# Three graph layers over sorted edges: chunks that begin at any stored record, and table steps written out

## The reference, cut to what matters

```
def _spmm(row, col, vals, x):
    msg = vals[:, None] * x[col]
    return jax.ops.segment_sum(msg, row, num_segments=N)

def _layer(x_prev, row, col, vals, W_a, b_a, W_b, b_b):
    h = _spmm(row, col, vals, x_prev)
    z = (h + x_prev) @ W_a.T + b_a + h * x_prev @ W_b.T + b_b
    return jnp.where(z >= 0, z, NEG_SLOPE * z)

x = emb[x_ids]; x1 = _layer(x, ...); x2 = _layer(x1, ...); x3 = _layer(x2, ...)
return jnp.concatenate((x, x1, x2, x3), axis=1)
```

## Time and profile before

| | us |
|---|---|
| median of 3 runs | 10225.11 (10217.66 to 10225.59) |
| profiled execution, its own time | 10220.25 |
| its span, first to last instruction | 10218.3 |
| TensorE matmuls busy | 9241.7 (90%) |
| VectorE busy | 8226.2 (81%) |
| GpSimd busy | 5098.6 (50%) |
| ScalarE busy | 4417.4 (43%) |
| mean granted TensorE clock | 0.92 |

### The profile page before, as it was taken

How to read it: one execution, slowest core, us unless ns; L and a number is a source line. 1 busy time by engine, 2 the same in 40 slices (tenths; PEclk the granted TensorE clock), 3 DMA queues, 4 the chain that set the end, 5 groups by cost and what they waited for, 6 DMA issues and landing times.

```text
span 10218.3 us, 236191 instructions
## 1 busy us (share of the span) xinstructions
PE 9241.7 (90%) x72184; PEld 8455.2 (83%) x72185; DVE 8226.2 (81%) x11648; ACT 4417.4 (43%) x13845; POOL 5098.6 (50%) x2843
## 2 busy tenths in 40 slices
PE   6788886788888669999999999999999999999999
PEld 4567665466676549999999999989999999999999
DVE  7899998699999857777777777777777777777777
ACT  0577775067777516652111256641111466511112
POOL 8477775057777500006888600028888200088885
PEclk8788887778888759999999999999999999999999
DMA  2111111011111299998888889998888699988885
GB/s 74 35 6 6 6 6 18 6 5 6 6 6 6 23 61 344 344 335 295 284 286 286 252 277 341 340 313 285 286 286 286 224 344 347 336 282 286 286 286 210
DMA packets 1121792, 1969.65 MB, mean 193 GB/s; under 512 B 390740, under 2 KB 442008, under 8 KB 1121080
## 3 DMA queue, kind: packets, MB, share of 16 engines
q0 software_dynamic: 399392, 1034.26, 32.8%
q1 hardware_dynamic: 722328, 934.52, 30.9%
HBM read 1212.58 MB, written 755.66 MB: 193 GB/s over the span
## 4 chain that ended last, share of the span: by engine, by line
PE 48%; DVE 20%; DMA 15%; issue 10%; ACT 3%; SPq 1%; DVEq 1%; POOL 0%; ACTq 0%; POOLq 0%
PE ps L912 35%; DMA messages<-work 14%; PE ps L903 7%; DVE hT L1102 7%; DVE place L1081 7%; DVE hT L1096 3%; ACT work L670 3%; PE ps L746 1%; PE ps L883 1%; PE ps L940 1%; PE ps L920 1%; PE ps L941 1%; PE ps L768 1%; DVE place L1086 0%; DVE place L1084 0%
## 5 line engine op out<-in xcount | busy, mean ns | idle before, releaser
L511 POOL DMA_INDIRECT work<-messages,work x1920 | 2923.1, 1522 | 3687.7 <-issue 3686.8
L912 PE MATMUL ps<-work 128*128 128x125 f32 x30720 | 3548.7, 278 | 38.3 <-DVE work L1279 38.3
L912 PEld LDWEIGHTS ps<-work 128*128 128x128 f32 x30720 | 3504.3, 192 | 82.7 <-DVE work L1279 39.4
L486 POOL DMA_INDIRECT sorted_edges<-stage,run_idx x798 | 1968.5, 2467 | 1286.1 <-ACT stage L615 570.9
L903 PE MATMUL ps<-xb,work 125*128 x21504 | 2459.2, 277 | 149.0 <-DVE work L1251 80.3
L903 PEld LDWEIGHTS ps<-xb,work 125*128 125x128 f32 x21504 | 2425.6, 193 | 182.6 <-issue 182.1
L1279 DVE TENSOR_TENSOR work<-work,iota_p 128x1000 f32<-128x1000 f32 x1920 | 2291.5, 1193 | 34.7 <-ACT work L688 34.7
L670 ACT ACTIVATE work<-ps,work 128x128 f32<-128x128 f32 x5376 | 1515.5, 372 | 1264.9 <-DMA messages<-work 648.5
L688 ACT ACTIVATE work<-work 128x8 f32<-128x8 f32 x1920 | 577.7, 301 | 2880.4 <-DMA work<-messages,work 2880.4
L796 PEld LDWEIGHTS ps<-hT 128*128 128x128 f32 x12768 | 1694.7, 215 | 69.4 <-issue 46.5
L626 ACT ACTIVATE hT<-iota_p,place 128x128 f32<-128x128 f32 x4788 | 1427.9, 386 | 707.7 <-DVE place L1086 699.7
(11 more groups left out here) (201 smaller groups left out, 3820.8 us busy)
## 6 DMA issues: line engine op xcount, KB each, us to landing
messages<-work SPq DMA_DIRECT2D x2688, 256.0 KB, 6.2
work<-slot_cols SPq DMA_DIRECT2D x672, 256.0 KB, 6.0
work<-messages,work POOLq DMA_INDIRECT x1920, 5.9
out_x<-xb SPq DMA_DIRECT2D x150, 125.0 KB
sorted_edges<-stage,run_idx POOLq DMA_INDIRECT x798, 3.7
work<-lane_places SPq DMA_DIRECT2D x532, 5.2 KB
out_x<-xb SPq DMA_DIRECT2D x4, 1562.5 KB
sorted_edges<-hT SPq DMA_DIRECT2D x4, 908.0 KB
```

The source lines that it names most:

```text
L486: pool.indirect_dma_start(out=sorted_edges[p], out_offset=bass.IndirectOffsetOnAxis(ap=run_idx[:, q, k:k + 1], axis=0), in_=stage[:, q, k ...
L511: pool.indirect_dma_start(out=ck[:, n, :, :].rearrange("p h x -> p (h x)"), out_offset=None, in_=octs, in_offset=bass.IndirectOffsetOnAxis ...
L912: last = t.matmul(part[n], ck[:, n, j // CH, j % CH * D:(j % CH + 1) * D], sel[:, n % SELB, j, :], start=j == 0, stop=j == CHB - 1)
```

## The change

- A chunk may begin at any stored record. The messages are seen as rows of 4 floats (`flat`), and ScalarE multiplies the chunk's index, now counted in records, by 129 (REC // CH) when it copies it. Each gather still brings 128 pieces of two records. The number of chunks of a pair is its number of records touched, halved and rounded up; the table counts records, the step from chunk to chunk is HALVES = 2, the limit of the `min` is CHUNKS in place of OCTS.
- A column block's groups in the second pass keep room for 4 more slots (`p * CH`), so that a chunk's second record is never another block's first. The number of groups stays at 896.
- TB becomes 592.
- Differences in the chunk table are split in three parts (4096, 64, 1) in place of two.
- The steps of both run tables are written out on VectorE and TensorE, with constant addresses, in four buffers (SCREDIT = 4). The steps of the chunk table are written out too, 296 steps of CR = 2 tiles in CQ = 2 buffers, in place of 128 steps of 5.

The diff, changed lines only:

```diff
@@ -49,6 +49,7 @@
+SCREDIT = 4
@@ -80,18 +81,18 @@
-OCTS = CHUNKS * CH // CHB
-TB = -(-((E + 2 * (CHB - 1) * NB * NB) // CHB // P + 1 + NB) // (2 * BU)) * 2 * BU
+TB = -(-((E + (2 * (CH - 1) + CH) * NB * NB) // CHB // P + 1 + NB) // (2 * BU)) * 2 * BU
+assert CHB == 2 * CH and (E + NB * (CH + GE - 1)) // GE <= GROUPS
-CR = 5
+CR = 2
-assert ABODIES * ZC >= N and ABODIES * ZC == 12544 and TB == 640 and GROUPS % AU == 0 and AU == CB * BATCH and AU % MR == 0
+assert ABODIES * ZC >= N and ABODIES * ZC == 12544 and TB == 592 and GROUPS % AU == 0 and AU == CB * BATCH and AU % MR == 0
@@ -188,8 +189,8 @@
-        run_step = wb[0:NBD, 2 * STEP0:2 * STEP0 + 2 * SPARE].rearrange("b (q x) -> b q x", q=2)
-        RT0 = STEP0 + SPARE
+        run_step = wb[0:NBD, 2 * STEP0:2 * STEP0 + SCREDIT * SPARE].rearrange("b (q x) -> b q x", q=SCREDIT)
+        RT0 = STEP0 + SCREDIT * SPARE // 2
@@ -263,8 +264,8 @@
-        delta_t = hb[0:NBD, 2 * (TS0 + CQ * CR * P // 2):2 * (TS0 + CQ * CR * P // 2) + 2 * TB].rearrange("c (t h) -> c t h", h=2)
-        assert TS0 + CQ * CR * P // 2 + TB <= ABODIES * ZC
+        delta_t = hb[0:NBD, 2 * (TS0 + CQ * CR * P // 2):2 * (TS0 + CQ * CR * P // 2) + 3 * TB].rearrange("c (t h) -> c t h", h=3)
+        assert TB // 4 * 3 <= 512 and TB % (4 * CR * CQ) == 0 and TS0 + CQ * CR * P // 2 + 2 * TB <= ABODIES * ZC
@@ -354,7 +355,6 @@
-        SCREDIT = 2
@@ -496,7 +496,7 @@
-            octs = messages.rearrange("(c h) f -> c (h f)", h=HALVES)
+            flat = messages.rearrange("c (u e) -> (c u) e", e=CH)
@@ -509,7 +509,7 @@
-                                out=ck[:, n, :, :].rearrange("p h x -> p (h x)"), out_offset=None, in_=octs,
+                                out=ck[:, n, :, :].rearrange("p h x -> p (h x)"), out_offset=None, in_=flat,
@@ -678,7 +678,7 @@
-                    s.activation(idx[:, h * BU:(h + 1) * BU], chunk_idx[:, at], ACT.Copy).then_inc(idx_ready, 1)
+                    s.activation(idx[:, h * BU:(h + 1) * BU], chunk_idx[:, at], ACT.Copy, scale=float(REC // CH)).then_inc(idx_ready, 1)
@@ -762,15 +762,12 @@
-                def step(w, q):
+                for w in range(W):
-                        last = t.matmul(ps[:, k, bass.ds(w * 2, 2)], run_step[:, q, k * P:(k + 1) * P],
-                                        delta[:, bass.ds(w, 1), :].rearrange("b a h -> b (a h)"), start=True, stop=True)
+                        last = t.matmul(ps[:, k, w * 2:w * 2 + 2], run_step[:, w % SCREDIT, k * P:(k + 1) * P], delta[:, w, :],
+                                        start=True, stop=True)
-
-                pairs(pe, 0, W // 2, lambda i, q: step(i * 2 + q, q))
-                step(W - 1, 0)
@@ -874,16 +871,13 @@
-            for b in range(4):
-                with pe.Fori(0, TB // 4 // CR // CQ) as j:
-                    for q in range(CQ):
-                        pe.wait_ge(cstep_ready, j * CQ + (b * (TB // 4 // CR) + q + 1))
-                        for r in range(CR):
-                            n = q * CR + r
-                            last = t.matmul(ps[:, b, bass.ds(j * (2 * CQ * CR) + 2 * n, 2)], chunk_step[:, q, r, :],
-                                            delta_t[:, bass.ds(j * (CQ * CR) + (b * (TB // 4) + n), 1), :].rearrange("c a h -> c (a h)"),
-                                            start=True, stop=True)
-                        last.then_inc(cstep_used, 1)
+            for k in range(TB // CR):
+                pe.wait_ge(cstep_ready, k + 1)
+                for n in range(k * CR, (k + 1) * CR):
+                    b, c = n // (TB // 4), n % (TB // 4)
+                    last = t.matmul(ps[:, b, 3 * c:3 * (c + 1)], chunk_step[:, k % CQ, n % CR, :], delta_t[:, n, :],
+                                    start=True, stop=True)
+                last.then_inc(cstep_used, 1)
@@ -981,7 +975,7 @@
-            for k, at in enumerate((DUMPS[0], DUMPS[1], OCTS)):
+            for k, at in enumerate((DUMPS[0], DUMPS[1], CHUNKS)):
@@ -1025,7 +1019,7 @@
-                rounded(marks[0:NBD, 0:1], lane_to[:, U - 1:U], (unit - 1) / 2, 1.0 / unit)
+                rounded(marks[0:NBD, 0:1], lane_to[:, U - 1:U], (unit - 1) / 2 + p * CH, 1.0 / unit)
@@ -1054,13 +1048,10 @@
-                def step(w, q):
+                for w in range(W):
-                    v.tensor_scalar(run_step[:, q, :], iota_run, tab("start_run")[:, bass.ds(w, 1)], None,
+                    v.tensor_scalar(run_step[:, w % SCREDIT, :], iota_run, tab("start_run")[:, w:w + 1], None,
-
-                pairs(dve, 0, W // 2, lambda i, q: step(i * 2 + q, q))
-                step(W - 1, 0)
@@ -1179,9 +1170,10 @@
-            rounded(m[3], m[1], -(CHB - 1) / 2, 1.0 / CHB)
-            rounded(m[4], m[2], (CHB - 1) / 2, 1.0 / CHB)
+            rounded(m[3], m[1], -(CH - 1) / 2, 1.0 / CH)
+            rounded(m[4], m[2], (CH - 1) / 2, 1.0 / CH)
+            rounded(m[5], m[5], (HALVES - 1) / 2, 1.0 / HALVES)
@@ -1214,24 +1206,26 @@
-            link(v.tensor_tensor(split(tt[2]), ps[0:NBD, 2:4, 0:TB // 2], split(tt[1]), ALU.subtract))
+            link(v.scalar_tensor_tensor(split(tt[2]), split(tt[1]), -float(HALVES), ps[0:NBD, 2:4, 0:TB // 2], ALU.mult, ALU.add))
-            rounded(tt[4], tt[3], 0.0, 1.0 / QHI)
-            v.tensor_scalar(delta_t[:, :, 0], tt[4], QHI, None, ALU.mult)
-            link(v.scalar_tensor_tensor(delta_t[:, :, 1], tt[4], -QHI, tt[3], ALU.mult, ALU.add))
-            with dve.Fori(0, TB // CR // CQ) as j:
-                for q in range(CQ):
-                    dve.wait_ge(cstep_used, j * CQ + (q + 1))
-                    v.tensor_tensor(chunk_step[:, q, :, :], iota_p[0:NBD, :][:, None, :].to_broadcast([NBD, CR, P]),
-                                    tt[1][:, bass.ds(j * (CQ * CR) + q * CR, CR)][:, :, None].to_broadcast([NBD, CR, P]),
-                                    ALU.is_ge).then_inc(cstep_ready, 1)
+            for k, part_ in enumerate((4096.0, 64.0)):
+                rounded(tt[4], tt[3], 0.0, 1.0 / part_)
+                link(v.tensor_scalar(delta_t[:, :, k], tt[4], part_, None, ALU.mult))
+                link(v.scalar_tensor_tensor(tt[3], tt[4], -part_, tt[3], ALU.mult, ALU.add))
+            link(v.tensor_copy(delta_t[:, :, 2], tt[3]))
+            for k in range(TB // CR):
+                dve.wait_ge(cstep_used, k + 1)
+                v.tensor_tensor(chunk_step[:, k % CQ, :, :], iota_p[0:NBD, :][:, None, :].to_broadcast([NBD, CR, P]),
+                                tt[1][:, k * CR:(k + 1) * CR][:, :, None].to_broadcast([NBD, CR, P]),
+                                ALU.is_ge).then_inc(cstep_ready, 1)
-                                 ps[:, 0:4, 0:TB // 2].rearrange("p k (t h) -> p k t h", h=2), AX.X, ALU.add))
+                                 ps[:, 0:4, 0:TB // 4 * 3].rearrange("p k (t h) -> p k t h", h=3), AX.X, ALU.add))
-            v.tensor_scalar(chunk_idx, chunk_idx, iota_c[:, :], float(OCTS), ALU.add, ALU.min).then_inc(tabs_done, 1)
+            link(v.scalar_tensor_tensor(chunk_idx, iota_c[:, :].to_broadcast([P, TB]), float(HALVES), chunk_idx, ALU.mult, ALU.add))
+            v.tensor_scalar(chunk_idx, chunk_idx, float(CHUNKS), None, ALU.min).then_inc(tabs_done, 1)

```

## The result

The kernel after takes 9883.96 us (median of 4 runs, 9876.09 to 9889.07), the kernel before 10223.46 us (4 runs on the same chip): ratio 0.9668, 95% interval 0.9651 to 0.9685. The forecast was 9867 us, 0.17% under it, and the time lies in its own range. It is right in sum, but by steps that were off in both directions, so the closeness is in part luck, and of rival B the place came true. The profiled execution after is 9886.18 us, its span 9884.4; before 10220.25 and 10218.3.

A forecast was written before the change was run, and what follows sets the result against it. TensorE bounds the tile stages, DMA the messages; table steps matter in the preparation. From 10220.25 us, -266.1 - 46 - 52 + 6 = -358 gives 9862, 9867 as a median; own range 9838 to 9915, high end with rivals 9950.

The forecast's parts named there:

- rival B: First sort: the written-out first run table starves the x0 gathers, +25 us, 19 more than forecast, 9886 us; chance 0.15.
- Tiles: Line 912, three layers: 640 tiles become 592, so 144 go at 1.848 us each, gaining 266.1 us.
- nothing else comes late in their place: Tile stages: real tiles keep size and count, so no new delay while a gather stays under 1.848 us of DMA time.
- Second run table: Second sort: 135 written-out steps at 0.40 us, 54 us in place of 100.2, a gain of 46.
- The lower bound: Second run table: 0.33 us a step, from the first two VectorE steps, which wait for nothing; gain 56 us.
- First run table: First sort: faster steps gain nothing, but may disturb the x0 gathers beside them, 6 us later.
- today's steps cost a gather 0.13 us only: First run table: argument against rival B, that the existing steps delay x0 gathers by just 0.13 us.
- Chunk table: Before the layers: 296 written-out steps at 0.50 us, 148 us in place of 203.5; gain 52, range 5 to 66.
- the round trip of a buffer: Chunk table: VectorE step, wait, two products and return take 1.04 us, so 0.52 a step with two buffers.
- the cap named in the forecast: Chunk table: first slot columns land at 3717.6 us behind the row numbers' transfer, limiting the gain to 66 us.
- Rival A: All tables: the written-out steps bring nothing and only the tiles count, 9965 us; chance 0.10.
- rival C: Tile stages: 16-byte chunk starts and view make the gather the bound, slower than before past f = 1.32; chance 0.03.

The follow-up runs named there:

- e1: Kernel after with all three tables as hardware loops again, keeping 592 tiles and the start at any record: 10052.61 us, ratio 0.9784.
- e2: Kernel after with only the first run table back in a hardware loop with two buffers: 9916.52 us, ratio 0.9649.
- e7: Kernel after, but in the first run table VectorE waits at every fourth step for all of TensorE's steps: 9932.16 us.
- e3: Kernel after with the stores of x0 moved behind the first sort's record load: 9864.5 us, ratio 0.9602.
- e8: Kernel after with the x0 stores moved as in e3 and the row numbers' transfer sent from ScalarE's queue: 9842.82 us, ratio 0.9574.
- e12: As e8, but the row numbers' transfer starts only once the three small tables are back: 9771.64 us on a third chip, ratio 0.9562.
- e9: Kernel after, unchanged, run on another chip as reference for the other runs there: 9960.9 us, ratio 0.9689.
- e4: Kernel before with the gathers' source viewed in pieces of 16 bytes, all addresses the same: 10281.68 us, kernel before 10277.23.
- e6: Kernel after with the first run table's comparison as a tensor_tensor in place of a tensor_scalar: 9986.5 us.

## Why the prediction was right

**Tiles, forecast -266.1, measured -250.4.** The count, the filler and 1.848 us a tile were right: e1 has 1094.5 us. Missing was a cost that I had put at nothing, 0.15 us at each turn of a rolled loop that merely stands elsewhere: 37 turns make 5.5 us a layer. The premise that "nothing else comes late in their place" failed by 0.5%.

**Second run table, -46, measured -55.3.** The direction and the cause hold; the step is 0.33, not 0.40. I sized it by three weight loads of 0.38 us together that in the new code take 0.16: in the trace of before register instructions of 0.046 us stand between these loads (792 for the 798 loads of line 768), so part of that row was the loop's own work. The lower bound, the distance of two steps that wait for nothing, was the true price.

**First run table, +6, measured +32.4.** This step failed, and rival B came true in place and nearly in price (+25). Not as worked out: no gather got slower by a share, a single one was held for the whole table. That rival's time, 9886, lies 2 us from the measured median, and that is luck too: its mechanism was another, and the terms beside it were off. e2 and e7 show that without gapless steps it does not happen, e3 that its cost passes only through SyncE's order, stores of x0 ahead of lane_places. My "today's steps cost a gather 0.13 us only" was read from a loop with gaps and carried over to one without.

**Chunk table, -52, measured -68.5.** I took 0.50 a step and it is 0.367. The term that was too large is the round trip of a buffer, which I put at 1.04 us: with two buffers at 0.367 it is at most 0.73. (My upper bound of 0.66 for the step is 0.64 by its own working, two products of 1.59 / 5.) The step alone would have given 22 us more: the cap named in the forecast, 66 by the first slot columns, is what came, 2 us better because their load landed after 153.4 us in place of 155.6. e8 and e12 show that the cap was the 16-byte transfer ahead of them.

**The sum.** Against the forecast: first sort +26.4, second run table -9.3, chunk table -16.5, tiles +15.7, and +7.8 in stages that I had at nothing (sorts, messages, dense), in all +24 on the profiled executions (9862 and 9886). Two steps too timid hid two losses; the losses and those stages alone come to 50 us. Rival A is refuted (e1 is the tiles alone, 92 us above e9, of which some 38 are its chunk loop, slower than before's), rival C too (e4, and share 0.85).

## What to carry to other kernels

When steps in a loop are written out, price them by the engine's own distance between steps that wait for nothing, and take the gaps they lose as something that another engine may have lived on: here 0.33 us in every four steps was enough for GpSimd's gathers, and none was not. Code that moves can change the pace of a loop that nobody touched, so compare the untouched stages too. Then ask what the faster stage runs into, here a transfer of 114,688 pieces of 16 bytes ahead of a small load in the same queue. Moving it to another queue gave more once it also started when nothing small was on the path (e12 against e8).

## What the runs showed of the hardware that I had not expected

- One indirect gather on GpSimd stood 32.44 us beside VectorE steps of 0.34 us, while the six ahead of it, beside the same steps, took 1.26 us each. In all nine traces with this table written out and no gaps it was the same gather, the 79th, after GpSimd's pause of 3 us, and it ended 1.1 us after the last step (47.08 us beside slower steps, e6).
- The turn of a rolled loop depends on where its code stands: 1.94, 1.98 or 2.10 us for the same instructions, not steadily with the distance (0 and 128 instructions more are alike, 64 is not). The delay comes in two steps of about 0.1 us, one behind the last add and one behind the branch.
- Stores of 2.5 to 3.5 KB beside a transfer of 16-byte pieces took 10.7 to 15.9 us to land, although that one has a queue of its own (e8); before it starts they took 1.4 to 1.8 (e12).
